# A two-expert feed-forward block on one core: row tiles kept as fp16 halves and turned by transposing DMAs instead of by TensorE

## What is computed

```python
x = x + tanh(g_xattn[0]) * xattn(layernorm(x), ctx_512, Wq, Wkv_expand, Wout)
n = layernorm(x)                                  # the second normalisation
weights, idx = top_k(softmax(n @ gate_w.T), 2)    # two experts of eight for each row
g = silu(n @ w1[e].T) * (n @ w3[e].T)             # up products, e = 0 .. 7
y = sum over a row's two experts of weight * (g @ w2[e].T)
z = (silu(n @ ws1.T) * (n @ ws3.T)) @ ws2.T       # shared expert
out = x + tanh(g_ffn[0]) * (y + z)
```

## Time and profile before

| | |
|---|---|
| median of 3 runs | 525.69 us (525.18 to 526.63) |
| the profiled execution's own time | 525.32 us |
| its span, first to last instruction | 523.5 us |
| TensorE busy | 435.4 us, 83% of the span |
| VectorE, ScalarE, GpSimd busy | 62%, 47%, 46% |
| mean granted TensorE clock | 0.947 of full speed |
| attention and shared expert | about 0 to 305 us |
| last lists, weights and first gather | about 305 to 324 us |
| expert stage | about 324 to 512 us |

### The profile page before, as it was taken

The page is one execution under the profiler, slowest core; times in us unless marked ns, Lnnn a source line. Parts: engine busy times, 40 slices in busy tenths (PEclk is TensorE's granted clock), DMA queues, the critical chain, the costliest instruction groups (busy, mean ns, idle before and its releaser), DMA issues. The chain is left out here.

```text
span 523.5 us, 8113 instructions
## 1 busy us (share of the span) xinstructions
PE 435.4 (83%) x2432; PEld 233.2 (45%) x2433; DVE 322.2 (62%) x641; ACT 246.0 (47%) x425; POOL 240.2 (46%) x185
## 2 busy tenths in 40 slices
PE   2699699988999889987756723999999999999991
PEld 1355455554555545544323311454555455455540
DVE  4798768887588865898888952343434343434330
ACT  4877554563356534486733611333433444333430
POOL 4008235405544154466583633255455455555532
PEclk9999789999999999999895975999999999999996
DMA  8970001120011100325649554166666665756652
GB/s 310 418 307 1 0 1 41 41 81 2 1 60 42 60 0 0 117 105 180 242 121 258 131 113 112 30 108 115 120 104 104 114 120 87 123 112 104 121 75 42
DMA packets 26375, 55.31 MB, mean 106 GB/s; under 512 B 9136, under 2 KB 9264, under 8 KB 25712
## 3 DMA queue, kind: packets, MB, share of 16 engines
q0 software_dynamic: 9760, 20.49, 22.2%
q1 hardware_dynamic: 16592, 34.54, 20.3%
HBM read 31.51 MB, written 23.50 MB: 105 GB/s over the span
## 5 line engine op out<-in xcount | busy, mean ns | idle before, releaser
L1288 PE MATMUL bank<-arena 128*128 128x512 f16 (+1 forms) x576 | 111.0, 350 | 3.2 <-issue 1.5
L1288 PE MATMUL bank<-arena,GT 128*128 x468 | 109.2, 384 | 0.2 <-issue 0.2
L521 POOL DMA_INDIRECT out<-Y,entry x39 | 61.6, 1579 | 84.0 <-ACT Y L787 41.1
L1288 PE MATMUL bank<-arena,gT 128*128 (+1 forms) x330 | 81.3, 383 | 5.4 <-DVE gT L810 4.9
L1288 PEld LDWEIGHTS bank<-arena 128*128 128x128 f16 x576 | 56.3, 99 | 52.6 <-issue 5.8
L536 ACT ACTIVATE arena<-bank 128x512 f16<-128x512 f32 (+1 forms) x88 | 49.8, 586 | 50.9 <-PE bank L1288 31.3
L1288 PEld LDWEIGHTS bank<-arena,GT 128*128 128x128 f16 x468 | 46.3, 99 | 48.3 <-issue 2.9
L810 DVE TENSOR_TENSOR GT<-bank,GT 128x512 f16<-128x512 f32 x39 | 27.0, 692 | 61.0 <-ACT GT L536 61.0
L452 POOL TENSOR_TENSOR arena<-arena,rd 128x1024 f32<-128x1024 f32 x16 | 30.5, 1905 | 52.3 <-DVE rd L923 52.3
L1288 PEld LDWEIGHTS bank<-arena,gT 128*128 128x128 f16 x330 | 32.1, 98 | 42.3 <-DVE gT L810 4.6
L1252 DVE SCALAR_TENSOR_TENSOR uu<-th,bank 128x256 f32<-128x256 f32 x39 | 16.4, 421 | 55.8 <-ACT th L772 55.8
(11 more groups left out here) (126 smaller groups left out, 602.2 us busy)
## 6 DMA issues: line engine op xcount, KB each, us to landing
x_sb<-in_experts SPq DMA_DIRECT2D x16, 768.0 KB, 6.0
xrows<-xn SPq DMA_DIRECT2D x16, 256.0 KB, 2.1
out<-x_sb SPq DMA_DIRECT2D x16, 256.0 KB, 2.2
xrows<-Y SPq DMA_DIRECT2D x1, 2304.0 KB, 24.5
out<-Y SPq DMA_DIRECT2D x1, 2304.0 KB, 28.6
x_sb<-in_x SPq DMA_DIRECT2D x2, 1024.0 KB, 9.1
x_sb<-in_x SPq DMA_DIRECT2D x1, 2048.0 KB, 16.4
arena<-in_wq SPq DMA_DIRECT2D x1, 1024.0 KB, 9.3
```

The source lines that it names most:

```text
L521: nc.gpsimd.indirect_dma_start(out=out, out_offset=bass.IndirectOffsetOnAxis(ap=entry[:, j, 0:1], axis=0), in_=Y[:, j % RING, :], in_offse ...
L1288: last = nc.tensor.matmul(dst, a, b, start=n == 0, stop=n == len(steps) - 1)
```

## The change

The rows of the second normalisation are split to two fp16 halves as they stand (`rows_half`: `hi` on ACT, `lo` on DVE, both from SBUF to SBUF into `xnh`), before anything turns them. A transposing DMA on SP's queue then writes `x2T` (128 rows of 1024 fp16 values to 8 blocks of 128x128), in place of TensorE's turn and of the halves' reading from PSUM. `xrows` holds both halves of a row, 2 x 512 fp16, which is as many bytes as 512 fp32 values had. In the expert stage a gathered tile is already two halves, and a transposing DMA on SP's queue turns it into `GT`. The order on TensorE becomes: up product of tile j+2, turn of `gg` of tile j+1, down product of tile j. `gT` has three buffers instead of two, `xnh` lies in the bytes of `Y` and half of `G`. The diff at its core:

```diff
-        xrows = nc.dram_tensor("xrows", (ROWS, D), F32)
+        xrows = nc.dram_tensor("xrows", (ROWS, 2 * D), F16)
...
             def store_rows(b):
                 for i in range(PER):
-                    sp.wait_ge(xn2_ready, 4 * b + i + 1)
...
+                    sp.wait_ge(x2_lo, 4 * b + i + 1)
+                    row = xnh[:, i].rearrange("p h d -> p (h d)")
+                    pass_waits(sp)
+                    sp.dma_start_transpose(x2T[:, :, :, i * P:(i + 1) * P].rearrange("p h c t -> p (h c) t"),
+                                           row).then_inc(x2_turned[i], 16)
+                    sp.dma_start(xrows[bass.ds((4 * b + i) * P, P), :], row).then_inc(st_rows, 16)
...
-            for j in range(TILES):
+            def turn_rows(j):
+                s = j % RING
+                sp.wait_ge(ld_rows[s], 16 * (j // RING + 1))
+                if j >= RING:
+                    sp.wait_ge(eh_mm, j - RING + 1)
+                sp.dma_start_transpose(GT[:, s].rearrange("p h c t -> p (h c) t"), G[:, s]).then_inc(e_turned[s], 16)
+
+            def watch(j):
+
                 sp.wait_ge(added[j % RING], 16 * (j // RING + 1))
                 sp.sem_inc(landed, 1)
                 if j + AHEAD < TILES:
                     load_list(j + AHEAD)
+
+            for j in range(RING):
+                turn_rows(j)
+            for j in range(TILES):
+                if j + RING < TILES:
+                    turn_rows(j + RING)
+                if j > 0:
+                    watch(j - 1)
+            watch(TILES - 1)
...
+            def gather_after(j):
+                pool.wait_ge(e_turned[j % RING], 16 * (j // RING))
+                gather(j)
+
+            gather_after(RING)
+            pool.wait_ge(st_base, 16 * NT)
             for j in range(TILES):
                 if j + RING + 1 < TILES:
-                    pool.wait_ge(eT_mm, j + 2)
-                    gather(j + RING + 1)
+                    gather_after(j + RING + 1)
                 add_rows(j)
...
+            def rows_half(b, i):
+
+                act.wait_ge(xn2_ready, 4 * b + i + 1)
+                act.wait_ge(st_init, 48)
+                if not isinstance(b, int) or b > 0:
+                    act.wait_ge(st_rows, 64 * b)
+                    act.wait_ge(x2_turned[i], 16 * b)
+                hi(xnh[:, i, 0, :], xn2[:, i * D:(i + 1) * D]).then_inc(x2_hi, 1)
...
+            def rows_half(b, i):
+
+                dve.wait_ge(x2_hi, 4 * b + i + 1)
+                lo(xnh[:, i, 1, :], xn2[:, i * D:(i + 1) * D], xnh[:, i, 0, :]).then_inc(x2_lo, 1)
```

More of the change, by code:

```diff
@@ L252, in turn_no @@
                 p_at = (2, 3, 5, 6, 8, 9, 10, 11) if last else range(2 * PER, 4 * PER)
-                at = i if kind == "x2" else PER + {"g": g_at, "x": range(1, 2 * PER, 2), "p": p_at}[kind][i]
-                start = 4 * PER + 5 * PER * (b - 1)
+                at = {"g": g_at, "x": range(1, 2 * PER, 2), "p": p_at}[kind][i]
+                start = 4 * PER + 4 * PER * (b - 1)
                 if isinstance(b, int) and b == B:
@@ L286, in turn_halves @@
             else:
-                dst = [(x2T if kind == "x2" else xTv)[:, h, :, i * P:(i + 1) * P] for h in range(2)]
+                dst = [xTv[:, h, :, i * P:(i + 1) * P] for h in range(2)]
             n = dst[0].shape[1]
@@ L508, in _ @@
             pool.wait_ge(st_rows, 16 * NT)
+            for i in range(PER):
+                pool.wait_ge(x2_turned[i], 16 * B)
             for j in range(RING):
                 gather(j)
-            pool.wait_ge(eT_mm, 1)
-            gather(RING)
-            pool.wait_ge(st_base, 16 * NT)
             def add_rows(j):
@@ L789, in step @@
                                      ).then_inc(ey_ready, 1)
+            def step(it, s, two=True, one=True):
+                j = RING * it + s
+                if two:
+                    tanh_e(j + 2, (s + 2) % RING)
+                if one:
+                    g_hi(j + 1, (s + 1) % RING)
+                scaled(it, s)
             split_piece(15)
-            rows_hi(0, 0)
-            rows_hi(1, 1)
             tanh_e(0, 0)
+            tanh_e(1, 1)
+            g_hi(0, 0)
             for s in range(RING):
@@ L800, in _ @@
             for s in range(RING):
-                step(ROUNDS - 1, s, turn=s == 0, nxt=s < 2)
+                step(ROUNDS - 1, s, two=s == 0, one=s < 2)
         @block.vector
@@ L1047, in feed_forward @@
                 head_max(c, 3)
+                rows_half(f, 2)
+                rows_half(f, 3)
                 hidden(f, 0)
-                turn_lo(c, "x2", 2)
-                turn_lo(c, "x2", 3)
                 hidden(f, 1)
@@ L1557, in step @@
                 turn(e_g, gg[:, s, :], IC).then_inc(egT_mm, 1)
-                if isinstance(j, int) and j == 0:
-                    for k in range(PIECES - 4, PIECES):
-                        pe.wait_ge(w_split[w_slot(k)], w_round(k))
-                if nxt:
-                    hidden_e(j + 1, (s + 1) % RING, e_next)
+            def step(it, s, two=True, one=True):
+                j = RING * it + s
+                e = expert_of(j)
+                if two:
+                    hidden_e(j + 2, (s + 2) % RING, it + (s + 2) // RING, expert_of(j + 2))
+                if one:
+                    turn_g_e(j + 1, (s + 1) % RING)
                 pe.wait_ge(egT_lo, j + 1)
@@ L1575, in _ @@
                 pe.wait_ge(w_split[w_slot(k)], w_round(k) - 1 + (e + 2) // E)
-            hidden_e(0, 0, e)
+            hidden_e(0, 0, 0, e)
+            for k in range(PIECES - 4, PIECES):
+                pe.wait_ge(w_split[w_slot(k)], w_round(k))
+            hidden_e(1, 1, 0, expert_of(1))
             pe.wait_ge(base_ready, NT)
+            turn_g_e(0, 0)
             for s in range(RING):
@@ L1583, in _ @@
             for s in range(RING):
-                step(ROUNDS - 1, s, turn_=s == 0, nxt=s < 2)
+                step(ROUNDS - 1, s, two=s == 0, one=s < 2)
 def kernel(**inputs):
```

129 lines of the change are left out of this document (51 added, 78 removed).

## The result

The changed kernel takes 628.2 us (median of 4 runs, 624.13 to 632.52) against 526.16 us before: a ratio of 1.194, 95% interval 1.185 to 1.203. It is slower, as forecast, and inside the range given (540 to 645), but the loss is 102 us where 46 were forecast, more than twice as much.

A forecast was written before the change was run, and what follows sets the result against it. It took TensorE to bound the expert stage, and a loop through the transposing DMA to bind after the change. 525.3 + 31 (stage) + 6 (middle batches) + 9 (last batch) = 571 us, 572 on the median; range 540 to 645.

The forecast's parts named there:

- What bounds the kernel: Old kernel: TensorE busy 83% of the span, and 38.96 of 40 us in an expert-stage window.
- the loop beside it: Expert stage: down product, Y, add, gather, landing take 7.96 us of the 9.08 available, 1.0 us to spare.
- the stage's +31: Expert stage: 218.7 us against 188.0, from a step of 5.65 us where the old one was 4.54.
- L: Time from a transposing DMA's issue to its landing, taken as 3.1 us, midway between 2.1 and 4.2.
- busy, not the bound: Expert stage: DMA engines would be busy at most 5.1 us of each 5.65 us step.
- The step's formula: Expert stage: step is the larger of 4.11 and (8.2 + L)/2 us, giving 5.65.
- Middle batches: Three batches beside attention: hidden(f,1) starts later behind a transposing DMA, +2.1 us each, +6 in all.
- Last batch: Transposing DMAs wait in SP's queue behind the load of piece 11; router's last logits at 291.0 against 282.0, +9 us.
- As fast as a plain copy: Rival: L = 2.1 us everywhere, stage +13, batches +3, last batch +8, 549 us in all; chance 0.14.
- Dear transposes: Rival: L of 6 us and more because of eight blocks; 660 us at L = 7, over 800 at 13.6; chance 0.19.
- The faster rival: Expert stage: the loop does not bind, the stage gains 17 us, about 514 us in all; chance 0.05.

The follow-up runs named there:

- early gathers: The changed kernel with POOL's gather of tile j+5 ahead of the add of tile j, and SP seeing landed adds one tile later: 561.41 us, ratio 1.069.

## Why the prediction was right in sign and wrong in size

- **What bounds the kernel, and the loop beside it: right.** The 7.96 us from the down product to the landing of the gather stand in the new trace as 8.04, and moving the gather (with SP's wait for adds) took 69 us off the stage.
- **The step that failed: the stage's +31, in which L was 3.1 and the DMA engines were "busy, not the bound".** L is 3.1 where the DMA engines are free. But the chain of waits of the changed kernel passes through 12 transposing DMAs in the stage, between 4.41 and 9.01 us long, 6.1 in the mean. I had weighed the engines' work against the mean step, and the work doesn't come evenly: POOL issues the adds and gathers of three tiles between 528.05 and 541.1, and the transposing DMA on which TensorE waits is under way from 534.20 to 542.42, with a DMA share of 1.03. A mean share of 0.66 says nothing on that.
- **The clock was left out.** It had no term for the stage, nor for the waits of 5 us that I forecast beside attention; I used 5.26 us for a product after a long idle time only in the last batch. In the stage the first up product of a round is 1.9 us longer than 2.75 (4.64 in the mean of the 12 that the chain shows from 382 us on). Work in the waits gave back 16 us in the stage and 8 us beside attention.
- **The step's formula was wrong, the other way, and by luck hid a part of the miss.** The wait stands ahead of the up product and shifts the down product behind it too, so the loop closes over three tiles and holds one step's work: 3 steps = 8.2 + L + 4.1. With L = 3.1 that is 5.14 a step, not 5.65, and +12 us for the stage, not +31; the whole forecast would have been about 553. With the chain's L of 6.1 and the 1.9 for the clock a round is 20.3, and 13 rounds are 264, measured 261.8. So the two costs that I left out are 3.0 and 1.9 us a round, 39 and 25 us over 13 rounds, and an error of 0.5 a step hid a part of them; with the right formula alone the forecast would have been further off.
- **Middle batches: +15.4 where +6 was forecast.** With work in the waits they cost 6.5 us (277.47 against 271.02), as forecast for the DMA; the rest, 8 to 9 us, is the clock by the same run. In the changed kernel the first products start 4.1, 8.0 and 14.2 us later than before in the three batches, and `norm2` of the last batch 15.4.
- **Last batch: about right**, +11.1 against +9. The first two transposing DMAs were slower than I took: TensorE goes on at 301.76, 5.2 us after the first one's issue at 296.53. The load of weight piece 11 stands right ahead of them in SP's queue, and from 296.5 to 299.8 the DMA engines moved nothing but its long packets (0.71 of its 0.79 MB):

```profile
DMA packets 115, 0.71 MB, mean 214 GB/s; under 512 B 0, under 2 KB 0, under 8 KB 115
```

- **Not in the sum:** +2.4 ahead of the first up product, where the chain now has a transposing DMA of 3.6 us (349.31 to 352.92) behind the first gather.
- **The rivals.** "As fast as a plain copy" was tried as such in the stage, 603 us where I gave 549 for all places: the same errors. "Dear transposes" was half right, since L was 6, but not for the eight blocks: alone, a DMA of eight blocks takes 3.1. The faster rival needed L under 0.9, and never had it.
- **The pages' rules.** The Trainium skill, page "Advanced Engine Details and Errata", section "X-Bar Transpose (TRN2)", has transposing DMAs as fast as regular ones. One transfer of 256 KB is slower here: 3.1 against 2.5 us for a store in the same trace. The Trainium skill, page "VectorE: DVE Perf Modes", section "The three transpose paths", gives 1309 ns for one 128x128 block by DMA. My estimate from it, 10.5 us for eight in turn, doesn't hold: eight take 3.1.

What stays open: L grew with POOL's traffic on the same engines, as the two windows of queues show, but no run holds the traffic and changes its moment only.

## What to carry to other kernels

A turn on TensorE costs engine time and is there when it is asked for; a transposing DMA costs a latency in whatever loop it is put, so look first for the loop (who frees the buffer, who is ahead of the gather in its queue) and count over how many tiles it closes before you count what TensorE saves. A DMA share of 0.6 is a mean: ask what else is on the engines at the moment when the critical transfer is issued. And a wait of some 5 us ahead of TensorE was paid twice here, once as wait and once in the matmuls behind it (7.39 us for 24 of them instead of 5.35). When an experiment reorders an engine's work, look at what else moved with it: the load of one number, put in the open, is my reading of 17 us of waits in one of these runs.

## What I had not expected of the hardware

A transposing DMA of 128 rows of 1024 fp16 values, alone, lands 3.1 us after its issue and holds SP's sequencer for 1.24 us, against 2.5 and about 0.5 for a store of the same bytes; all 55 in the changed kernel are seen in the page as 67,216 packets under 512 B instead of 9,136. In the stage 39 of them make the DMA engines' busy time 0.66 x 263 = 174 us instead of 0.59 x 188 = 111, 1.6 us a tile. The windows of the stage, before, changed, and with early gathers:

```profile
324.00:512.00 188.00, 181.59 (x929) 93.71 (x928) 72.25 (x155) 71.55 (x154) 94.39 (x73) 0.99 0.59 102
```

```profile
353.00:616.00 263.00, 188.61 (x780) 85.02 (x780) 46.00 (x117) 52.80 (x117) 94.75 (x74) 0.85 0.66 110
```

```profile
351.00:544.00 193.00, 171.23 (x779) 80.79 (x780) 46.01 (x117) 52.04 (x116) 93.81 (x73) 0.95 0.87 149
```

And 312 matmuls that nobody reads made a kernel 16 us faster (611.92 against 628.2 us).
